# Half of the last mixture is routed and scattered within the latent attention, and its shared expert stands behind the tiles

## The reference

```python
def _L3_ffn_ref(x, Wg, Ws1, Ws3, Ws2, We1, We3, We2):   # x: 4096 tokens of 128
    gates = jax.nn.sigmoid(xf @ Wg)                      # 8 experts
    vals, idx = jax.lax.top_k(gates, 2)
    vals = vals / vals.sum(axis=-1, keepdims=True)
    w = jnp.zeros((T, E), x.dtype).at[jnp.arange(T)[:, None], idx].add(vals)
    shared = jax.nn.silu(xf @ Ws1) * (xf @ Ws3) @ Ws2    # 256 hidden
    h = jax.nn.silu(jnp.einsum('td,edf->tef', xf, We1)) * jnp.einsum('td,edf->tef', xf, We3)
    routed = jnp.einsum('tef,efd,te->td', h, We2, w)
    out = (shared + routed) / 3
...
x = x + jnp.tanh(g_xattn[3]) * _L3_xattn_ref(ctx_1024, _layernorm(x, axis=-1), ...)
x = x + jnp.tanh(g_ffn[3]) * _L3_ffn_ref(_layernorm(x, axis=-1), ...)
```

## Time and profile before

| | |
|---|---|
| device time, three runs | 1998.58, 2000.26, 5949.81 us; median 2000.26 |
| the profiled execution | 1994.44 us, its span in the trace 1992.4 us |
| granted TensorE clock, mean | 0.888 |
| busy of the span | PE 77%, DVE 54%, POOL 39%, ACT 34% |
| attention of layer 3, loop | from about 1240 to 1645 us, 32 steps |
| the last mixture | 1645 us to the end at 1992.4 us |
| weights of a tile (layer 3) | 384 KB, its rows 128 KB |
| indirect DMAs on POOL | 128 scatters, 128 gathers over both mixtures |

### The profile page before, as it was taken

One profiled execution on the slowest core, in us unless ns is written; L12 is line 12 of the kernel. 1 busy time (PEld: TensorE's weight loads), 2 busy tenths in 40 slices (PEclk: granted clock), 3 DMA queues, 4 the chain that ended last, 5 costly groups with the idle time before them and its releaser, 6 DMA issues. The chain is left out here.

```text
span 1992.4 us, 32964 instructions
## 1 busy us (share of the span) xinstructions
PE 1539.1 (77%) x10543; PEld 1196.2 (60%) x10543; DVE 1077.0 (54%) x2403; ACT 667.6 (34%) x1657; POOL 779.3 (39%) x1037
## 2 busy tenths in 40 slices
PE   2999971499925686888878887899999995279990
PEld 2777751398924554666654445777777774148880
DVE  3666662022436976677767884555555546024462
ACT  1555530032303332444442332444444441011110
POOL 1444417501453444334333331444444432710146
PEclk9999975699965597999998998999999996679995
DMA  8000002477710000000000000000000001216772
GB/s 279 1 0 0 0 1 72 124 211 214 225 50 6 1 1 1 1 0 0 0 1 0 0 0 1 1 0 0 0 0 0 0 0 35 86 36 180 204 223 66
DMA packets 90840, 100.47 MB, mean 50 GB/s; under 512 B 11156, under 2 KB 73804, under 8 KB 90125
## 3 DMA queue, kind: packets, MB, share of 16 engines
q1 hardware_dynamic: 53490, 69.07, 11.4%
q0 software_dynamic: 8192, 16.79, 3.0%
q10 hardware_dynamic: 29083, 13.66, 2.4%
HBM read 70.92 MB, written 28.57 MB: 50 GB/s over the span
## 5 line engine op out<-in xcount | busy, mean ns | idle before, releaser
L395 POOL TENSOR_TENSOR exp_scores<-exp_scores,softmax_recip 128x308 f32<-128x308 f32 x256 | 181.7, 741 | 268.7 <-DVE softmax_recip L506 268.7
L716 POOL DMA_INDIRECT gathered_rows_ffn<-sorted_y,slot_ffn x128 | 120.9, 944 | 326.9 <-DMA sorted_y<-expert_rows_ffn 253.9
L989 PE MATMUL psum<-sorted_transposed_ffn,tile_weights_ffn 128*128 128x256 f32 x736 | 186.6, 398 | 28.8 <-issue 24.6
L989 PEld LDWEIGHTS psum<-sorted_transposed_ffn,tile_weights_ffn 128*128 128x128 f32 x736 | 136.9, 196 | 54.6 <-issue 27.3
L1598 POOL TENSOR_TENSOR exp_scores_xattn<-exp_scores_xattn,softmax_recip_xattn 128x1640 f32<-128x1640 f32 x32 | 93.5, 2923 | 192.4 <-DVE softmax_recip_xattn L1724 192.4
L705 POOL DMA_INDIRECT sorted_x<-xn_ffn,slot_ffn x128 | 122.9, 960 | 113.0 <-DVE slot_ffn L850 74.6
L524 PE MATMUL psum<-identity,exp_scores 128*77 128x128 f32 x1024 | 147.9, 282 | 15.7 <-POOL exp_scores L395 12.7
L589 PE MATMUL psum<-probs_transposed,v_padded 77*32 77x128 f32 x2048 | 135.9, 275 | 17.6 <-ACT probs_transposed L410 17.3
L410 ACT COPY probs_transposed<-psum 77x512 f32<-77x512 f32 x192 | 109.6, 586 | 117.0 <-PE psum L524 116.8
L998 PE MATMUL psum<-tile_weights_ffn,hidden_ffn 128*128 128x128 f32 x1104 | 141.4, 279 | 1.7 <-issue 1.7
L524 PEld LDWEIGHTS psum<-identity,exp_scores 128*77 128x77 f32 x1024 | 115.6, 149 | 36.5 <-POOL exp_scores L395 21.4
(11 more groups left out here) (316 smaller groups left out, 3315.6 us busy)
## 6 DMA issues: line engine op xcount, KB each, us to landing
tile_weights_ffn<-in_L_ffn_packed_dram SPq DMA_DIRECT2D x46, 512.0 KB
tile_weights_ffn<-in_L_ffn_packed_dram SPq DMA_DIRECT2D x46, 384.0 KB
sorted_rows_ffn<-sorted_x SPq DMA_DIRECT2D x92, 128.0 KB
sorted_y<-expert_rows_ffn ACTq DMA_DIRECT2D x92, 128.0 KB
sorted_x<-zeros SPq DMA_DIRECT2D x4, 1472.0 KB, 13.9
x_residual<-in_x_dram SPq DMA_DIRECT2D x4, 512.0 KB, 11.6
sorted_x<-xn_ffn,slot_ffn POOLq DMA_INDIRECT x128
gathered_rows_ffn<-sorted_y,slot_ffn POOLq DMA_INDIRECT x128
```

The costliest lines, as they stand in the source:

```text
L395: nc.gpsimd.tensor_tensor(e[:, par, heads, :], e[:, par, heads, :], rec.to_broadcast([S, HG, KC]), ALU.mult).then_inc(s["probs_ready"], 1)
L716: nc.gpsimd.indirect_dma_start(yg[:, n % 4, k, :], None, m.sorted_y[half][:, :], bass.IndirectOffsetOnAxis(slot[:, half, k, b:b + 1], 0)). ...
L989: mm = nc.tensor.matmul(m.psum[:, 2 * (n % 2) + half, c * TILE:(c + 1) * TILE], w[:, n % DEPTH, at:at + 128], xst[:, n % 2, :], start=True ...
```

## The change

1. `pipeline` gets a parameter `looped`; `latent_attention` sets it to 16, so that only steps 2 to 15 are looped and steps 16 to 29 are written out.
2. The tensors of the routing move into an object `Routing` that for layer 3 is allocated before the attention and lives through both phases. Picking, placing and the tiles' experts become functions of their own. The counts of earlier picks are now first copied from PSUM to `before_in_batch` (one copy more a half, in both mixtures).
3. In layer 3's attention half 0 (batches 0 to 15) is routed within steps 17 to 21: VectorE's variance ahead of the row maxima of step 17 and the normalisation at its end, transposes and logits on TensorE in steps 18 to 20, the picks at the end of VectorE's step 20, counts and slots in step 21. From step 22 on GpSimd issues three scatters behind each step's probabilities, 32 in all up to step 32.
4. The mixture of layer 3 begins with one half placed (`PLACED = 1`): it normalises and routes groups 4 to 7 only, and scatters half 1 only. TensorE's first tile waits for the slots of half 1, no more for the shared expert.
5. The shared expert stands behind the tiles on TensorE, ScalarE and VectorE. The last 16 combines are woven into it, two behind each group's addition from the second on. SyncE's stores of the output wait for the shared sums as well.
6. In layer 0's attention the projections move behind the shift matmuls. Layer 2's attention keeps its order.

The tasks of the functions `pick_experts`, `place_in_slots` and `expert_of_tiles` are the lines L812 to L855 as they stood, with the extra copy. The core of the diff:

```diff
 def pipeline(eng, step, n=B, looped=None):
+    looped = n - 2 if looped is None else looped
     step(-1, 1, True, False, False)
     step(0, 0, True, True, False)
     step(1, 1, True, True, True)
-    with eng.Fori(0, (n - 4) // 2) as i:
+    with eng.Fori(0, (looped - 2) // 2) as i:
         step(i * 2 + 2, 0, True, True, True)
         step(i * 2 + 3, 1, True, True, True)
+    for i in range(looped, n - 2):
+        step(i, i % 2, True, True, True)
...
 # head_attention, TensorE step
+                    if over_heads:
+                        projections(b, par, nxt, front, middle)
...
+                    if not over_heads:
+                        projections(b, par, nxt, front, middle)
...
 # sparse_experts
+    PLACED = 1 if layer == 3 else 0
+    FIRST_GROUP = PLACED * PGROUPS
...
+                        if shared:
+                            sync.wait_ge(s["shared_added"], g + 1)
...
-                for half in range(HALVES):
-                    pool.wait_ge(s["ranked"], half + 1)
+                for half in range(PLACED, HALVES):
+                    pool.wait_ge(s["ranked"], half + 1 - PLACED)
...
+                    pick_experts(nc, m, r, half, link, s["picked"])
+                    dve.wait_ge(s["counted"], half + 1 - PLACED)
+                    nc.vector.tensor_copy(r.before[:, :, :], counts_of(half, 0).rearrange("p (b e) -> p e b", e=E0))
+                    link(nc.vector.tensor_copy(r.total[:, :, :], counts_of(half, 1).rearrange("p (b e) -> p e b", e=E0)))
+                    place_in_slots(nc, m, r, half, link, s["ranked"])
+                    expert_of_tiles(nc, m, r, half, link, s["tiles_known"])
...
 # VectorE, behind the tiles
+                if shared:
+                    dve.wait_ge(s["scale_ready"], 1)
+                    for g in range(NGB + 1):
+                        if g < NGB:
+                            for c in range(chunks):
+                                dve.wait_ge(s["shared_silu"], g * chunks + c + 1)
+                                if g >= 2:
+                                    dve.wait_ge(s["shared_y"], g - 1)
+                                nc.vector.tensor_tensor(shid[:, g % 2, c, :], ssilu[:, c, :], m.psum[:, 2 + c, :], ALU.mult).then_inc(s["shared_hid_ready"], 1)
+                        if g >= 1:
+                            dve.wait_ge(s["shared_y"], g)
+                            dve.wait_ge(s["combined"], B - HBATCH + max(0, g - 2) * 2)
+                            xg = m.x[:, (g - 1) * GB:g * GB, :].rearrange("p b d -> p (b d)")
+                            nc.vector.scalar_tensor_tensor(xg, m.psum[:, 4 + (g - 1) % 2, :], third[:, 0:1], xg, ALU.mult, ALU.add).then_inc(s["shared_added"], 1)
+                            if g >= 2:
+                                dve.wait_ge(s["shared_added"], g)
+                                combine(B - HBATCH + 2 * g - 4)
+                                combine(B - HBATCH + 2 * g - 3)
+                    for n in range(B - 2, B):
+                        combine(n)
...
 # TensorE
-                    pe.wait_ge(s["shared_added"], NGB)
-                pe.wait_ge(s["ranked"], HALVES)
+                count_picks(HALVES - 1)
+                pe.wait_ge(s["ranked"], HALVES - PLACED)
...
+                    pe.wait_ge(s["hidden_ready"], NTILES)
+                    shared_up(0)
+                    for g in range(1, NGB):
+                        shared_up(g)
+                        shared_down(g - 1)
...
 # latent_attention
+        ROUTE = HBATCH + 1
+        SCATTER = ROUTE + 5
+        PER_STEP = 3
...
 # GpSimd, behind the probabilities of the step
+                    if isinstance(b, int) and b >= SCATTER:
+                        pool.wait_ge(s["route_ranked"], 1)
+                        for pair in range((b - SCATTER) * PER_STEP, min((b - SCATTER + 1) * PER_STEP, 2 * HBATCH)):
+                            nc.gpsimd.indirect_dma_start(m.sorted_x[0][:, :], bass.IndirectOffsetOnAxis(r.slot[:, 0, pair % 2, pair // 2:pair // 2 + 1], 0),
+                                                         r.xn[:, pair // 2, :], None).then_inc(scattered, 16)
+
+                assert (B + 1 - SCATTER) * PER_STEP >= 2 * HBATCH
+                pipeline(pool, step, looped=HBATCH)
...
 # ScalarE
+                    if isinstance(b, int) and b == ROUTE:
+                        act.wait_ge(s["route_var"], 1)
+                        nc.scalar.activation(m.sd[:, 0:HBATCH], m.var[:, 0:HBATCH], ACT.Sqrt, bias=m.eps[:, 0:1]).then_inc(s["route_sd"], 1)
+                        preload(nc, m, ACT.Exp)
+                    if isinstance(b, int) and b in (ROUTE + 1, ROUTE + 2):
+                        for g in range(0, 3) if b == ROUTE + 1 else range(3, 4):
+                            act.wait_ge(s["route_xt_in_psum"], g + 1)
+                            nc.scalar.copy(r.xts[:, g * GT:(g + 1) * GT], m.psum[:, 4 + g % 3, :]).then_inc(s["route_xts"], 1)
+                    if isinstance(b, int) and b == ROUTE + 3:
+                        act.wait_ge(s["route_logits"], 1)
+                        nc.scalar.activation(r.probs[:, 0, :, :], m.psum[:, 7, 384:384 + HBATCH * E0].rearrange("p (b e) -> p b e", e=E0), ACT.Exp,
+                                             scale=-1.0).then_inc(s["route_exp"], 1)
...
 # VectorE: ahead of the row maxima, behind them, at the end of the step
+                    if routing == 0:
+                        dve.wait_ge(s["route_moments"], 1)
+                        variance_of_x(nc, m, dve, s["route_parts"], s["route_var"], HBATCH)
...
+                    if routing == 4:
+                        dve.wait_ge(s["route_counted"], 1)
+                        nc.vector.tensor_copy(r.before[:, :, :], m.psum[:, 5, 0:HBATCH * E0].rearrange("p (b e) -> p e b", e=E0)).then_inc(s["route_counts_read"], 1)
+                        nc.vector.tensor_copy(r.total[:, :, :], m.psum[:, 5, HBATCH * E0:2 * HBATCH * E0].rearrange("p (b e) -> p e b", e=E0))\
+                            .then_inc(s["route_counts_read"], 1)
...
+                    if routing == 0:
+                        rstd_of_x(nc, m, dve, s["route_sd"], s["route_rstd"], s["route_shift"], HBATCH)
+                        for n in range(HBATCH):
+                            ins = nc.vector.tensor_scalar(r.xn[:, n, :], m.x[:, n, :], m.rstd[:, n:n + 1], m.shift[:, n:n + 1], ALU.mult, ALU.add)
+                        ins.then_inc(s["route_xn"], 1)
+                    if routing == 3:
+                        dve.wait_ge(s["route_exp"], 1)
+                        pick_experts(nc, m, r, 0, link, s["route_picked"])
+                    if routing == 4:
+                        dve.wait_ge(s["route_counts_read"], 2)
+                        place_in_slots(nc, m, r, 0, link, s["route_ranked"])
+                        expert_of_tiles(nc, m, r, 0, link, s["route_known"])
...
 # TensorE: ahead of the transposes of the next rows
+                        if routing == 2:
+                            for g in range(3):
+                                pe.wait_ge(s["route_xts"], g + 1)
+                                route_logits(g)
+                        if routing == 3:
+                            pe.wait_ge(s["route_xts"], 4)
+                            route_logits(3).then_inc(s["route_logits"], 1)
...
 # behind them
+                    if routing == 1:
+                        pe.wait_ge(s["route_xn"], 1)
+                        wait(pe, s["c_ready"], (b - 1) * 2)
+                        wait(pe, s["pt_read_dve"], (b - 1) * 2)
+                        for g in range(3):
+                            route_transposes(g)
+                        pe.wait_ge(s["route_xts"], 3)
+                    if routing == 2:
+                        wait(pe, s["c_ready"], (b - 1) * 2)
+                        route_transposes(3)
+                        pe.wait_ge(s["route_xts"], 4)
+                    if routing == 4:
+                        pe.wait_ge(s["route_picked"], 1)
+                        wait(pe, s["c_ready"], (b - 1) * 2)
+                        nc.tensor.matmul(m.psum[:, 5, 0:HBATCH * E0], m.earlier[:, :], r.either[:, 0, :], start=True, stop=True)
+                        nc.tensor.matmul(m.psum[:, 5, HBATCH * E0:2 * HBATCH * E0], m.all_ones[:, :], r.either[:, 0, :], start=True, stop=True)\
+                            .then_inc(s["route_counted"], 1)
...
```

More of the change, by code:

```diff
@@ L593, in _, with __init__, sb @@
                 pipeline4(pe, step)
-def sparse_experts(nc, m, sem, layer, router_t, packed, shared_weights, clear, out=None):
+class Routing:
+    def __init__(self, nc, ctx, layer):
+        def sb(name, shape, dtype=F32):
+            return ctx.enter_context(nc.sbuf_tensor(f"{name}_ffn{layer}", shape, dtype))
+        self.layer = layer
+        self.xn = sb("xn", [S, B, D])
+        self.xts = sb("xt", [D, B * S if layer == 3 else 2 * GT])
+        self.probs = sb("probs", [S, HALVES, HBATCH, E0])
```

(32 more changed lines are left out.)

326 lines of the change are left out of this document (153 added, 173 removed).

## The result

The changed kernel takes 1966.95 us (median of four runs, 1964.13 to 1970.87), the kernel before 1999.42 beside it: a ratio of **0.9846**, interval 0.9829 to 0.9863. One of the four executions of the kernel before took 5949.81 us; the others lie between 1995.89 and 2000.26, and ratios here are of executions like those. The profiled execution has a span of 1962.3 us against 1992.4, so 30.1 us less; 34 were forecast.

The account below looks back on a forecast made before the run. Between attention and expert tiles, back-to-back scatters were taken to starve every engine but GpSimd. 22 + 19 - 119 + 40 + 5 - 1 = -34 us on 1994.4 gave 1960.4, plus 5.9 to the median: 1966, range 1927 to 1997.

Parts of the forecast that it names:

- the stall: First tiles: half 1's 32 scatters beside them starve the engines, three tiles in 49.4 us, 40 us lost (bounds 5 and 45).
- Routing in the attention: Layer 3's attention, steps 17 to 21: routing half 0 there adds 22.3 us, bounds 12 to 30.
- Scatters in the attention: Steps 22 to 32: three scatters per step make it 14.8 us long; eight steps add 19 us, bounds 8 and 30.
- the 1.4 us of slack: Attention step: 1.4 us between the next context rows being ready and TensorE taking them, so 2.4 of 3.8 us stay.
- the 16 us that I had named as a sign of being wrong: Attention: the prediction falls if steps with scatters exceed 16 us.
- Earlier tiles and the stall: Last stage: tiles begin at 1673.6 instead of 1792.73, 119.1 us gained; half 1's scatters beside them lose 40 us.
- Tail: Shared expert behind the tiles: last tile's copy to end 56 us instead of 50.7, +5 us, bounds 0 and +30.
- Rival B: Tail: shared expert isn't hidden, goes in 10 us steps beside the gathers, 81 us instead of 56, 1991 us; chance 0.15.
- Layer 0: Layer 0's attention: projections behind the shift matmuls give -1 us, bounds -10 and +8.
- Rival A: First tiles: no starvation or a late one, loss 5 or 20 us instead of 40, put at 1938 us; chance 0.32.
- Rival C: Attention steps 22 to 32: starvation, one 10.5 us stall in each of 11 steps, 116 us, 2082 us; chance 0.08.

Follow-up runs that it names:

- the kernel that shows it by itself: Kernel without layers: small instructions on VectorE, ScalarE and TensorE beside scatters, gathers or plain transfers; under the stall a copy starts every 1.40 us, a transpose every 2.80.

## Why the prediction was right

The time was right within a microsecond of the median, and so was the mechanism, but that closeness is luck. On the profiled execution 1960.4 us were forecast and 1964.13 measured; the forecast added 5.9 us from there to the median, where it turned out 2.8. And within the sum, sizes were off against each other: the stall 8 us smaller than predicted, the attention 7, the tail 4 and the tiles' gain 4 us worse, the attention's start 3 better. Step by step, measured on the profiles (predicted in brackets):

- **Routing in the attention**: steps 16 to 21 are 25.4 us over 12.40 each (22). I had said 17 to 18 us for each; apart from the first (12.63) they are 13.08 to 20.26. The worst, 20.26, is the one with the 16 normalisations at its end, 4.63 us on VectorE directly ahead of the next row maxima, followed by transposes that TensorE waits 3.11 us for.
- **Scatters in the attention**: 21.9 us over 12.40, in steps 22 to 29 (19). Apart from the first the steps are 14.63 to 15.46 (14.8), which bears out the 1.4 us of slack; the run with the scatters ahead shows that GpSimd's order is the reason. The first, 17.11, is over the 16 us that I had named as a sign of being wrong; with the scatters ahead it is still 15.54, so most of its excess is not the scatters', and its cause stays open.
- **Earlier tiles and the stall**: from the last probabilities to the fifth tile's copy it was 180.0 us (1632.5 to 1812.5) and is 96.8 (1675.9 to 1772.7), so -83.2 (-119 + 40 = -79). Without scatters it is 65.2, so the stall costs 31.6 and not 40, and the rest -114.8 and not -119. VectorE was at work again 5 us after the last scatter and not 9, and nearly four tiles got through instead of three.
- **Tail**: from the last tile's copy 60.1 us (56), 50.7 before: 9.4 instead of 5, by the stops of 4.20 and 2.23 us. In the two kernels profiled on the chip without the stall, the same tail has no stops and takes 54.6 us, against the 54.4 that I had before I added most of a halt; so I put the 5.5 us more down to the stall. Rival B, 81 us, did not occur: the gathers wait for the combines, and two rows of eight passed in this tail without a stop. But they do not wait after eight at most, as I had thought: twelve came in a row, and both stops lie there.
- **Layer 0**: -3 us (-1); in the first profile layer 3's attention begins 4.4 us earlier than before, in the other profiles with the new order beside a stall 0.7 to 4.5 earlier and once 2 later, by chance of the run.

Sum: 25.4 + 21.9 + 0.5 - 83.2 + 0.3 + 9.4 - 4.4 = -30.1, the difference of the spans (0.5 is the attention's first steps, 0.3 the other tiles, 4.4 where the attention begins).

Rival A, a late or missing stall, is what the chip of 1897 us has: no variant of the changed kernel profiled there stalls, and the kernel before, though not profiled there, is 100 us faster too. Not all of that is the last mixture's: layer 3's attention begins at 1210 to 1211 us in the three profiles of that chip, and at 1245 to 1252 in all others, so some 35 us lie in earlier phases. Rival C, a stall in the attention, did not occur: the steps with three scatters behind the probabilities are longer by GpSimd's order alone.

The part that the prediction did not see is in its own sum. It credited 119 us to tiles that begin earlier and charged 41 to the attention and 40 to the stall, as if half 0's early placing were needed for that. With the shared expert moved and half 0 not placed early, the tiles could start after 32 scatters, inside the same stall, and come out of it at the same time: 0.986 against 0.985 and 0.9857. The gain comes from the shared expert's new place; the early routing and scattering just pay for themselves where the stall is. Where nothing stalls they cost 24 us with the shared expert back in its old place (1.0128). With it moved, the changed kernel was not run on such a chip; an estimate is 1866.6 plus 8 x 2.4, so 1886 us or 0.994, within 2 us of the 1883.87 without the early half. So they would pay for themselves there too, but no more.

## What to carry to other kernels

Before work is moved into a full pipeline to shorten a wait, ask what the wait ends on: here both ways led into the same stall, and 48 us spent in the attention brought back 48. Work slipped into an engine's list belongs where that engine waits (ahead of the probabilities, 12.24 us a step) and not behind its last deed of the step (14.7). And long rows of indirect transfers should be broken by short pauses, here in pairs, one pair to a tile: worth 29 us where the chip stalls (35 by the ratios), and within 2 us of having no scatters at all.

## What was not expected of the hardware

- On three of four chips, back-to-back indirect DMAs slow every engine but GpSimd. In the kernel that shows it by itself, run on one of the three, instructions then start whole multiples of about 0.70 us apart (a copy each 1.40, a transpose each 2.80), beside scatters and gathers alike, until 7 us after the last scatter. On the fourth chip nothing of it shows, and the kernel before takes 1897 instead of 2000 us there.
- The amount of traffic is not the cause: the scatters move 51 to 52 GB/s on both kinds of chip at a DMA share of 0.15, and 46 plain transfers at 62 GB/s don't stall.
- A written-out step of the attention takes 12.24 us, with three scatters in it, and also between its second and third probabilities, ahead of the loop, with none; a looped one takes 12.40.
